# Two graph-attention layers on one core: the adjacency loaded in pieces of 512 columns instead of 256

## The reference

```
x   : (4096, 64) float32       adj : (4096, 4096) int32 of 0 and 1, about 1 in 1024 set
for layer in (0, 1):
    h = x                       (layer 0)      h = x @ weight_w          (layer 1)
    e[i, j] = leaky(h[i] . a_src + h[j] . a_dst)          slope 0.01
    att     = softmax over j of (e where adj > 0, else a very large negative number)
    x       = layernorm(x + att @ h (+ bias in layer 1))
```

## Time and profile before

| what | value |
|---|---|
| median of three runs | 514.14 us (512.53 to 514.8) |
| the profiled execution's own time | 512.94 us |
| its span, first to last instruction | 511.1 us |
| busy: TensorE, VectorE, ScalarE | 87%, 78%, 78% |
| layer 0's loop | about 62 to 274 us |
| passage to layer 1 | about 262 to 306 us |
| layer 1 | to the end |

### The profile page before, as it was taken

One profiled execution on the slowest core, in us unless ns is written; L12 is line 12 of the kernel. 1 busy time (PEld: TensorE's weight loads), 2 busy tenths in 40 slices (PEclk: granted clock), 3 DMA queues, 4 the chain that ended last, 5 costly groups with the idle time before them and its releaser, 6 DMA issues.

```text
span 511.1 us, 11789 instructions
## 1 busy us (share of the span) xinstructions
PE 445.8 (87%) x4420; PEld 416.2 (81%) x4420; DVE 401.3 (78%) x712; ACT 397.5 (78%) x619; POOL 85.8 (17%) x68
## 2 busy tenths in 40 slices
PE   0799678979979798997969989999999999989891
PEld 0479668969978796997869869999999998989791
DVE  3679999889898998989887989775766657574854
ACT  2685279777998888789873749889898989898941
POOL 0002211415133051412403200000101010101010
PEclk9987978988999799898989859999999999999897
DMA  7999999999999999999953001102020111102000
GB/s 198 245 224 277 275 263 293 338 299 333 312 307 315 328 321 306 322 321 299 320 173 125 1 1 44 42 9 86 12 82 19 73 34 58 57 35 75 20 12 10
DMA packets 80294, 87.71 MB, mean 172 GB/s; under 512 B 7298, under 2 KB 76162, under 8 KB 80258
## 3 DMA queue, kind: packets, MB, share of 16 engines
q1 hardware_dynamic: 45602, 52.98, 36.3%
q10 hardware_dynamic: 34656, 34.21, 24.7%
HBM read 77.74 MB, written 9.44 MB: 171 GB/s over the span
## 4 chain that ended last, share of the span: by engine, by line
issue 50%; DVE 21%; DMA 21%; PE 3%; POOL 2%; SPq 1%; ACT 0%; POOLq 0%; ACTq 0%; DVEq 0%
DMA stage<-in_adj 19%; DVE narrow L791 5%; DVE turned L803 3%; PE acc L418 2%; DVE pos L817 2%; POOL small L968 2%; DMA xn<-in_x 2%; DVE num L861 1%; DVE num L854 1%; DVE red L847 1%; DVE kept L728 1%; DVE bn L866 1%; DVE kept L725 1%; DVE neg L820 1%; SPq L225 1%
## 5 line engine op out<-in xcount | busy, mean ns | idle before, releaser
L557 ACT ACTIVATE neg<-srow,dcol 128x512 int8 (+1 forms) x512 | 352.8, 878 | 11.7 <-issue 8.2
L418 PE MATMUL acc<-xy_old,pos 128*128 128x195 bf16 x1024 | 195.2, 260 | 26.3 <-POOL pos L979 22.1
L418 PE MATMUL acc<-xy_old,neg 128*128 128x195 bf16 x1024 | 195.0, 261 | 0.0
L418 PE MATMUL acc<-stage,pos 128*128 128x195 bf16 x1024 | 179.4, 249 | 4.8 <-DVE red L829 4.8
L418 PE MATMUL acc<-stage,neg 128*128 128x195 bf16 x1024 | 179.4, 249 | 0.0
L418 PEld LDWEIGHTS acc<-xy_old,pos 128*128 128x128 fp8e4 x1024 | 106.2, 104 | 34.8 <-issue 33.5
L418 PEld LDWEIGHTS acc<-stage,pos 128*128 128x128 fp8e4 x1024 | 101.2, 99 | 9.9 <-issue 9.7
L418 PEld LDWEIGHTS acc<-xy_old,neg 128*128 128x128 fp8e4 x1024 | 105.7, 103 | 1.4
L418 PEld LDWEIGHTS acc<-stage,neg 128*128 128x128 fp8e4 x1024 | 100.7, 98 | 0.2
L791 DVE TENSOR_SCALAR narrow<-stage 128x4096 uint8<-128x4096 int32 x32 | 74.0, 2314 | 17.7 <-DMA stage<-in_adj 16.9
L820 DVE TENSOR_TENSOR neg<-neg,kept 128x1024 uint32<-128x1024 uint32 x32 | 39.2, 1224 | 44.7 <-ACT neg L557 44.1
(11 more groups left out here) (117 smaller groups left out, 326.6 us busy)
## 6 DMA issues: line engine op xcount, KB each, us to landing
stage<-in_adj ACTq DMA_DIRECT2D x64, 512.0 KB, 9.1
stage<-in_adj SPq DMA_DIRECT2D x64, 512.0 KB, 9.4
spill<-turned SPq DMA_DIRECT2D x16, 512.0 KB, 8.1
turned<-spill SPq DMA_DIRECT2D x16, 512.0 KB, 3.9
out<-x1s SPq DMA_DIRECT2D x8, 128.0 KB, 1.9
xn<-in_x SPq DMA_DIRECT2D x1, 768.0 KB, 16.7
kept<-in_x SPq DMA_DIRECT2D x4, 128.0 KB, 3.8
kept<-in_x ACTq DMA_DIRECT2D x4, 128.0 KB, 4.6
```

Source lines behind the costliest of these rows:

```text
L418: last = nc.tensor.matmul(acc[:, r, c * XW:(c + 1) * XW], masks[c][:, t // BYTES, t % BYTES, r * P:(r + 1) * P], xy[layer][:, g * GT + t, ...
L557: last = nc.scalar.activation(o[:, t // BYTES, t % BYTES, :], srow[:, bass.ds((s % 2) * 512, 512)], ACT.Sign, bias=dcol[:, layer, col:col ...
```

## The change

A tile of the load becomes 256 rows by 2048 columns: each of its four DMAs (still 32 partitions, still 512 KB) takes 8 rows in pieces of 512 columns, 2 KB. Two tiles, n = 0 and 1 (or 2 and 3), hold the two halves of the rows of the same 2048 columns, so both must be turned before either of the two granules that they feed can be masked. A block takes every fourth row (`HS = 4`), and the rows of x are loaded four at a time. `mask` waits for the pair, `turn` writes half of each of four runs of the pair, and `spill_out` waits until all four `turn` of the super-row are done. The orders of VectorE, ScalarE and TensorE are written anew round this. VectorE's becomes:

with `mask(0,3)` in the place of `mask(s,2)` and no residual or moments at s = 0. The core of the diff:

```diff
+    PB = 2 * GB
+    JC = PB * P
+    HS = NA
+    LR = GR // 2
-        stage = sb("stage", [P, SLOTS, GR * JC], I32)
+        stage = sb("stage", [P, SLOTS, LR * JC], I32)
-            t = tensor.rearrange("(k m p h) d -> k h p m d", m=groups, p=p, h=2)
+            t = tensor.rearrange("(k m p h) d -> k h p m d", m=groups, p=p, h=HS)
+        def load(queue, quarters, s, n):
             rows = rows_of(adj, s, GR, Q)
+            m = n % 2 * LR
             for a in quarters:
+                c = n // 2 * (NA * JC) + a * JC
+                queue.dma_start(stage[Q * a:Q * a + Q, n % SLOTS, :].rearrange("p (m j) -> p m j", j=JC),
+                                rows[:, m:m + LR, c:c + JC]).then_inc(loaded[n % SLOTS], 16)
         def load_rows(queue, c):
-            queue.dma_start(xn[:, :, :].rearrange("p (c h) d -> p c (h d)", h=2)[:, c],
+            queue.dma_start(xn[:, :, :].rearrange("p (c h) d -> p c (h d)", h=HS)[:, c],
...
-            load_rows(sp, slice(RB, IB // 2))
+            load_rows(sp, slice(RB, IB // HS))
             def spill_out(s, g):
-                sp.wait_ge(turned_ready, s * NG + g + 1)
+                sp.wait_ge(turned_ready, s * NG + NG)
...
             def body0(s, first=False, near=False, last=False):     # TensorE
                 granule(0, s, NG - 1)
+                if last:
+                    pe.wait_ge(shift_ready, 3)
...
             def copy_x1(s):
-                nc.scalar.copy(xTs[0:D, :].rearrange("d (b n a q) -> d a b q n", a=NA, b=GB, q=Q),
+                nc.scalar.copy(xTs[0:D, :].rearrange("d (b a q) -> d a b q", a=NA, b=PB),
             def body0(s, first=False):                             # ScalarE
-                for g in range(1, NG):
+                for g in range(2, NG):
                     if g == NG - 1 and not first:
                         copy_x1(s - 1)
-                    signs(0, s + 1, g)
+                    signs(0, s + 1, g, range(0, GT // 2))
                     load_next(s + 1, g)
+                    signs(0, s + 1, g, range(GT // 2, GT))
-                signs(0, s + 2, 0)
-                load_next(s + 2, 0)
                 if not first:
                     copy_wh(s - 1)
+                for g in range(2):
+                    signs(0, s + 2, g, range(0, GT // 2))
+                    load_next(s + 2, g)
+                    signs(0, s + 2, g, range(GT // 2, GT))
                 normalize(0, s)
...
+            def turn(s, n):
+                k = s * NG + n
+                if n < 2:
+                    pair = kept[:, s * (KEEP * GN):(s + 1) * (KEEP * GN)]
+                else:
+                    pair = turned[:, :, :].rearrange("p g n -> p (g n)")
+                if n == 2 and s > 0:
+                    dve.wait_ge(pos_ready, s * NG)
+                    for g in range(NG - KEEP):
+                        dve.wait_ge(spilled[g], 16 * s)
                 dve.wait_ge(narrowed, k + 1)
+                to = words(pair).rearrange("p (b i) -> p b i", b=PB)[:, :, n % 2 * (GW // PB):(n % 2 + 1) * (GW // PB)]
+                nc.vector.transpose(to, words(narrow[:, 0:GN]).rearrange("p (b i) -> p b i", b=PB)).then_inc(turned_ready, 1)
             def mask(layer, s, g):
                 if layer == 0:
-                    dve.wait_ge(turned_ready, s * NG + g + 1)
+                    dve.wait_ge(turned_ready, s * NG + g // 2 * 2 + 2)
...
+            tables0(1)                                             # VectorE, the start
+            to_bytes(0, 1)
+            turn(0, 1)
             mask(0, 0, 0)
+            mask(0, 0, 1)
+            tables0(2)
+            to_bytes(0, 2)
+            turn(0, 2)
+            to_bytes(0, 3)
+            turn(0, 3)
+            mask(0, 0, 2)
+            tables0(3)
             row_factors0()
...
-            near_shift()
-            mask(0, NS - 1, NG - 1)
+            mask(0, NS - 1, 2)                                     # VectorE, after the loop
+            residual_sum(0, NS - 2)
+            mask(0, NS - 1, 3)
+            moments(0, NS - 2)
             dve.wait_ge(exp_ready, 5)
             near_tables(0)
```

More of the change, by code:

```diff
@@ L149, in gat_kernel @@
         s_psum0 = misc[:, 408:408 + IB]
[L150 removed]
+        s_psum1 = [misc[:, 408:408 + IB], flip[:, 256:256 + IB]]
         mean_psum = flip[:, 0:BYTES * D]
@@ L429, in turn_x1, with body0 @@
                 for b in range(RB):
-                    rows = s // 2 * (2 * RB) + s % 2 + 2 * b
+                    rows = s // HS * (HS * RB) + s % HS + HS * b
                     last = nc.tensor.transpose(flip[0:D, b * P:(b + 1) * P], xn[:, rows, :], idf[:, :])
                 last.then_inc(x1_turned, 1)
-            def body0(s, first=False, last=False):
+            def body0(s, first=False, near=False, last=False):
                 granule(0, s, NG - 1)
+                if last:
+                    pe.wait_ge(shift_ready, 3)
                 if not first:
@@ L449, in body0 @@
                     project(s - 1)
-                granule(0, s + 1, 1)
-                if last:
+                if near:
                     pe.wait_ge(xT_ready, NS + s)
                     turn_max(0)
+                granule(0, s + 1, 1)
+                if near:
                     spread_max(0)
@@ L462, in _ @@
             body0(0, first=True)
-            for s in range(1, NS - 2):
+            for s in range(1, NS - 3):
                 body0(s)
+            body0(NS - 3, near=True)
             body0(NS - 2, last=True)
             granule(0, NS - 1, NG - 1)
-            pe.wait_ge(shift_ready, 3)
             turn_x1(NS - 2)
@@ L508, in _, with load_next @@
             load(act, UPPER, 0, 0)
-            def load_next(s, g):
-                act.wait_ge(narrowed, s * NG + g + 1)
-                load(act, UPPER, s + (g + SLOTS) // NG, (g + SLOTS) % NG)
+            def load_next(s, n):
+                act.wait_ge(narrowed, s * NG + n + 1)
+                load(act, UPPER, s + (n + SLOTS) // NG, (n + SLOTS) % NG)
             def tables0():
@@ L607, in _ @@
             row_factors(0)
-            signs(0, 1, 0)
-            load_next(1, 0)
+            for g in range(2):
+                signs(0, 1, g)
+                load_next(1, g)
             body0(0, first=True)
@@ L710, in row_factors1 @@
                 step(nc.vector.tensor_tensor(drop[:, 0:1], minus_shift[:, 1, 1:2], minus_shift[:, 1, 0:1], ALU.subtract))
-                for part, n in enumerate((slice(0, 3 * IB // 4), slice(3 * IB // 4, IB))):
-                    last = nc.vector.tensor_scalar(scol[:, n], s_psum1[part], 1 - SLOPE, drop[:, 0:1], ALU.mult, ALU.add)
+                half = IB // 2
+                nc.vector.tensor_scalar(scol[:, 0:half], s_psum1[0][:, 0:half], 1 - SLOPE, drop[:, 0:1], ALU.mult, ALU.add)
+                for part in range(2):
+                    h = slice(2 * part, 2 * part + 2)
+                    last = nc.vector.tensor_scalar(
+                        scol[:, half:IB].rearrange("p (r h) -> p r h", h=HS)[:, :, h],
+                        s_psum1[part][:, half:IB].rearrange("p (r h) -> p r h", h=HS)[:, :, h],
+                        1 - SLOPE, drop[:, 0:1], ALU.mult, ALU.add)
                 step(last)
@@ L902, in _ @@
             turn(0, 0)
+            tables0(1)
+            to_bytes(0, 1)
+            turn(0, 1)
             mask(0, 0, 0)
-            for g in range(1, NG):
-                to_bytes(0, g)
-                turn(0, g)
-                tables0(g)
-                if g < NG - 1:
-                    mask(0, 0, g)
+            mask(0, 0, 1)
[6 more added lines that the diff above has]
+            tables0(3)
             row_factors0()
```

99 lines of the change are left out of this document (46 added, 53 removed).

## The result

The kernel after takes 534.51 us (median of four runs, 532.99 to 537.01), where the kernel before, run beside it, took 513.34 (four runs, 512.41 to 514.8): a ratio of 1.0415, interval 1.0365 to 1.0464. The profiled execution took 532.99 us, with a span of 531.2, where 512.94 and 511.1 were before. Predicted were 526.0, within 507 to 538.

A forecast was written before the change was run, and what follows sets the result against it. Layer 0's turn was bound by VectorE's own work, 27.9 us, with load waits 2.2 above it. Layer 0's read-out, 285.9, became 299.5 less 0.4: +13.1 on 512.94 gives 526.0 us, range 507 to 538.

The forecast's parts named there:

- The spill's new wait: Layer 0's loop: lower tile 1 issued 5.7 us later, with both spills; two stalls of 2.2, turn 32.2 us, 30.0 before.
- One sign failed: Expected sign in layer 0's loop: the DMA row shows gaps near each turn's end, SyncE's queue empty for almost 4 us.
- A lone queue at 200 GB/s: Layer 0's loads: one queue alone, filling one half of the partitions, moves 200 GB/s, bounds 175 and 243.
- Rival 1: Layer 0's loads: a lone queue reaches the 363 GB/s of both; turn 29.2, 508 us in all; chance 0.25.
- Larger pieces: Layer 0's loads: 2 KB pieces run at 363 GB/s with both queues full, 5.8 us a half-tile, bounds 5.5 and 6.0.
- Rival 3: Layer 0's loop: spills at 2.6 us and no gain from 2 KB; turn 34.9, 542 us; chance 0.11.
- Slow rows (rival 4): Layer 0's loads: all at 243 GB/s, as from an unlucky row pitch; 37 us a turn, 555 us; chance 0.03.
- The start: Before layer 0's loop: tables0(1) covers a wait of 2.35, x's larger load costs 0.8; turn 0 starts at 60.3.
- Turn 0: Layer 0's first turn: 23.7 us of work plus a stall of 1.9 for tile 2, ending at 85.9.
- Six turns: Rest of layer 0's loop: six turns of 32.2 us and 1.4 for small parts, ending at 280.7.
- the passage: From layer 0 to layer 1: TensorE runs three last granules unbroken, 16.8 us plus 0.9; read-out at 299.5, +13.6.
- layer 1: Second layer, which doesn't load the adjacency: its duration stays, only its starting time moves.

The follow-up runs named there:

- experiment 1: Kernel after with SyncE's lower half of tile 1 issued before both spills of the previous super-row: 513.57 us, 1.0002 of the kernel before.
- experiment 2: Kernel before with only the spill's wait made later, until all four turn of its super-row are done: 528.65 us, 1.0311.
- Experiment 5: Kernel after with average(s) moved behind turn(s+1,3) in VectorE's order: 530.77 us, 1.0325 of the kernel before.
- experiment 11: Experiment 1's kernel with each queue's two DMAs crossing the partition halves in the same order, so both begin in the same half: 575.1 us, 1.1202.
- experiment 3: Kernel after with each load DMA cut into two of 256 columns, 1 KB pieces: 542.01 us, 1.056 of the kernel before.
- experiment 4: Experiment 1's kernel with each load DMA cut into two of 256 columns, 1 KB pieces: 514.4 us, 1.0053 of the kernel before.
- experiment 7: Experiment 1's kernel with average moved behind turn(s+1,3), and to_bytes(0,2) and turn(0,2) ahead of tables0(2) in the start: 517.95 us, 1.0086.
- experiment 9: Experiment 1's kernel with the spill of granule 3 issued by ScalarE's queue instead of SyncE's: 514.96 us, 1.0024 of the kernel before.

## Why the prediction was right, and where its sizes were off

Its mechanism and its sign hold, its time is 7.0 us short of the profiled execution's (526.0 against 532.99). By its own steps:

- **The spill's new wait: right, and nearly in size.** Lower tile 1 was to land at 9.6 of the turn and tile 2 at 17.1. They are turned into bytes at 9.1 and 16.4 in one of the turns shown and at 10.3 and 17.6 in the next. Stalls of 2.2 + 2.2 = 4.4 a turn were predicted, 19.9 / 5 = 4.0 measured, and 32.2 for the turn where the five take 32.0. Experiments 1 and 2 show the step by itself, from both sides. One step inside it is not as worked out. The upper half of tile 2 was to join at 3.5 of the turn and leave the lower half of tile 1 with 181 GB/s. In the traces it joins at 7.4 to 7.7, and the lower half runs alone at about 215. The landing comes out nearly the same, so part of the good fit is luck. Experiment 5 points the same way: the halves coming one after the other is a part of the cost that the working has no term for.
- **One sign failed.** The DMA row was to have gaps near each turn's end, because SyncE's queue stands empty. It does, but ScalarE's alone keeps the share at 1.06 (218 to 221.6), and no gap shows.
- **A lone queue at 200 GB/s: right.** 208 and 215 in the stretches above. That this is the half of the partitions was argued from the earlier trace rows; experiment 11 shows it, but for the columns that are read together. Rival 1 (a lone queue at 363) falls with it. The Trainium skill, "SBUF — State Buffer", section "Door 1: The DMA port swizzle", puts one half at 196 GB/s measured and about 218 at most, and the 208 and 215 agree. The same page's section "Can I just issue two DMAs to hit both halves?" says no, with 6% gained in its own measurement; here the measurement decides otherwise, 387 GB/s from two queues in two halves beside 215 from one.
- **Larger pieces: the rate about right, the worth overrated in the end.** 363 GB/s was taken for both queues; stretches of 2 us in which both carry only loads show 353 (74 to 76) to 387. Rival 3's "no gain" is out for the kernel after (7.5 us, experiment 3) and all but true once the order is mended (experiment 4).
- **Slow rows (rival 4): out.** Stretches of 353 to 387 GB/s with a pitch of 2 MB leave no room for it. The low stretches shown are lone halves. The Trainium skill, "DMA: Bandwidth & Descriptors", section "Latency and other measured facts", has its 164 GB/s at a row pitch of 2 MiB for copies of 128 partitions x 16 KiB, with the pitch counted from partition to partition. Here the rows of neighbouring partitions lie 64 KB apart, and the 2 MB are between two rows of one partition. So it was no rule against this change, and no row of these loads shows its loss.
- **The start: the largest term that was off, +5.2.** Turn 0 was to begin at 60.3:

```profile
15.04 1.88 PE L319 MATMUL acc<-idf,xn 128*64 128x128 f32 x8 [15.04 <-DMA xn<-in_x]
...
20.63 1.24 DVE L739 TENSOR_TENSOR kept<-kept,wts 128x1040 f32<-128x1040 f32 x1 [0.60 <-ACT wts L543]
...
65.46 2.29 DVE L805 TENSOR_SCALAR narrow<-stage 128x4096 uint8<-128x4096 int32 x1
...
79.37 2.29 DVE L805 TENSOR_SCALAR narrow<-stage 128x4096 uint8<-128x4096 int32 x1 [4.88 <-DMA stage<-in_adj]
```

  x came 2.8 us later than in the earlier trace rows, where 0.8 was taken: 2.0 of the 5.2, inside the bound of 3. It differs from execution to execution: the ten traces with the whole load of 512 KB begin at 11.64 to 15.04, 13.3 on average, the three with 256 KB at 11.80 to 12.25, 12.1 on average. So the change costs about 1.3 here, and the trace of the kernel after has the latest start of the ten. Another 2.85 are three instructions of VectorE that took 0.95 us longer each beside GpSimd, a cost that the prediction had put at 0 (told below). 0.35 stays unexplained.
- **Turn 0: +3.3.** A stall of 1.9 was predicted, 4.88 measured. Experiments 1 and 7 leave it about as long (4.11 and 3.69), so neither the spills nor the order of the start makes it. While the tile is loaded both queues are at work, but from 70 to 74 they move only 0.49 and 0.48 MB, 242 GB/s, the rate of one half. Why is open.
- **Six turns: -1.7, the passage: +0.5, layer 1: -0.3.** TensorE starts its last three granules at 287.78 and the last read ends at 306.19 + 0.56 = 306.75: 19.0 us where 18.5 were worked out. They are busy without a break, at a clock of 0.91, and it is their chain that ends last, as predicted (VectorE's tables ended at 300.9):

```profile
287.78:306.20 18.42, 18.42 (x194) 18.17 (x195) 14.36 (x27) 8.27 (x15) 5.56 (x4) 0.91 0.32 116
```

  Layer 1 takes 531.2 - 306.75 = 224.5 us, 511.1 - 285.93 = 225.2 before.

Together 5.2 + 3.3 - 1.7 + 0.5 - 0.3 = 7.0. In the prediction's own terms its six turns end at 280.5, not at the 280.7 that it went on with. The read-out moved by 306.75 - 285.93 = 20.8 us, and layer 1 gave 0.7 of it back.

Experiment 1 adds what the prediction never worked out: the change with its order mended is worth nothing, 513.57 us against 512.57. Its loop is faster, 29.4 us a turn where 30.1 were (five turns each), but turn 0 begins 2.0 us later (63.83, 61.80 in the earlier trace rows) and waits 4.11 and 1.88 us for the adjacency, and 4.1 us of VectorE's work only moved from turn 0 to the passage, as the prediction had it. The last read ends at 287.37, 1.4 behind the kernel before.

## What to carry to other kernels

When a wait is made later on a queue that also carries loads, look at what is queued behind it: the loss is theirs, and putting the spill behind the load that is wanted next cost nothing here. A full DMA row is no proof of a full rate: look at the bytes of each queue in short stretches, and at which half of the partitions each one fills. Larger pieces pay only where the transfers are what is waited for, so find out first how much of a turn is left above the busiest engine's own work.

## What the runs showed of the hardware

**A half of the partitions is a limit of its own.** 208 and 215 GB/s go into one half by one queue (218 to 221.6 and 227 to 229 in the kernel after), and two queues that begin in the same half reach 243 on average, spills included (experiment 11). Two queues in two halves reach 326 on average, spills included (experiment 1), and 387 in a stretch of loads alone. The share of the DMA engines stands at 1.02 to 1.08 in all of them: packets take longer, and engines count as busy.

**A DMA can start late while the other queue is at work.** ScalarE's loads issued at 192.84 and 224.15 began to move at about 198 and 229, when SyncE's earlier load was nearly through. In experiment 2 the one issued at 191.22 began at about 196. Where nothing else was under way, data moved 1 us after the issue (51.25 and 52.2 in the kernel after). Only the traces show this; no run was made for it, and why it is so stays open.

**VectorE and GpSimd hold each other up.** VectorE in the kernel after, then GpSimd; columns as above:

```profile
38.85 1.23 DVE L840 TENSOR_TENSOR neg<-neg,kept 128x1024 uint32<-128x1024 uint32 x1
40.71 2.17 DVE L840 TENSOR_TENSOR neg<-neg,kept 128x1024 uint32<-128x1024 uint32 x1
44.07 1.65 DVE L741 CAST xy_old<-kept 128x1040 bf16<-128x1040 f32 x1
...
40.34 1.47 POOL L1012 TENSOR_TENSOR pos<-kept,neg 128x512 uint32<-128x512 uint32 x1 [39.88 <-DVE neg L840]
43.06 2.10 POOL L1012 TENSOR_TENSOR pos<-kept,neg 128x512 uint32<-128x512 uint32 x1 [1.26 <-DVE neg L840]
```

The same tensor operation takes 1.23 alone and 2.17 when it begins inside GpSimd's; the cast takes 0.70 alone and 1.65. What is left of each behind the end of GpSimd's is about its time alone: 42.88 - 41.81 = 1.07 of 1.23, 45.72 - 45.16 = 0.56 of 0.70; a third case, a cast at 59.42, took 1.66. GpSimd's own, 1.27 where it is alone (28.91 in the kernel before), grows to 1.47 and 2.10. Beside the 32-bit transposes, where the loop places it, GpSimd's takes 1.27 and the transpose 1.24: neither is held up. The Trainium skill, "SBUF — State Buffer", section "Who interferes with whom", has the rule: a VectorE instruction with two inputs in SBUF, or a cast in its fast form, and a GpSimd instruction that reads SBUF exclude each other for the whole instruction. The trace agrees, with 0.95 us each time. No run took it away, so its 2.85 us are read from the trace alone.

**Two more things stay open:** the wait of 4 to 5 us for the adjacency in turn 0, and the last 1 to 1.5 us of wait a turn in experiments 1 and 9, where both queues are full at some 327 GB/s and neither order nor balance moves it.
